# A two-layer decoder on one core: adapter scores of layer 0 issued for four groups of heads at once instead of two

## The reference

```python
# sliding-window attention, head dim 64, 8 key heads shared by 32 query heads
scores = q @ k.T * 64**-0.5 + sliding_mask          # causal, window 64
x = layernorm(x + softmax(scores) @ v @ w_out.T)
# adapter attention, head dim 8
scores  = q @ k.T / sqrt(8) + attention_mask
a_score = q @ a_k.T / sqrt(8)                       # a_k, a_v: from the context
out = softmax(scores) @ v + tanh(gate) * softmax(a_score) @ a_v
x = layernorm(x + out @ Wo)
# then 16 experts, 6 of them weighted per token, then layer 1
```

## Time and profile before

| | |
|---|---|
| Time, median of 3 runs | 1478.36 us (1475.77 to 1478.98) |
| Time of the profiled execution | 1475.77 us |
| Its span, first to last instruction | 1474.0 us |
| Mean granted TensorE clock | 0.903 of full speed |
| PE busy | 1293.9 us, 88% of the span |
| DVE busy | 1073.8 us, 73% |
| ACT busy | 687.0 us, 47% |
| Layer 0, heads phases | about 56 us in each of blocks 0 to 6, 38 us in block 7 |

### The profile page before, as it was taken

The page is one execution under the profiler, slowest core; times in us unless marked ns, Lnnn a source line. Parts: engine busy times, 40 slices in busy tenths (PEclk is TensorE's granted clock), DMA queues, the critical chain, the costliest instruction groups (busy, mean ns, idle before and its releaser), DMA issues.

```text
span 1474.0 us, 24416 instructions
## 1 busy us (share of the span) xinstructions
PE 1293.9 (88%) x9109; PEld 854.9 (58%) x9114; DVE 1073.8 (73%) x2477; ACT 687.0 (47%) x1286; POOL 102.2 (7%) x95
## 2 busy tenths in 40 slices
PE   3777999999999999999999999988899598898576
PEld 1544766766766776676676676656777322222334
DVE  3647668857857857857867865744888899999477
ACT  1323633633643543553453463432444388888242
POOL 1111011001002002001001100000000000000001
PEclk9997999999999999999999999999999855555689
DMA  8300100100200200010010013002000099999100
GB/s 334 122 11 12 60 12 15 60 12 11 64 12 4 71 12 5 24 48 12 15 60 12 12 60 115 19 22 93 8 9 5 1 182 176 176 182 171 30 1 29
DMA packets 174517, 83.96 MB, mean 57 GB/s; under 512 B 137920, under 2 KB 170048, under 8 KB 173888
## 3 DMA queue, kind: packets, MB, share of 16 engines
q1 hardware_dynamic: 173248, 82.03, 23.0%
q10 hardware_dynamic: 1152, 0.36, 0.1%
HBM read 43.57 MB, written 5.24 MB: 33 GB/s over the span
## 4 chain that ended last, share of the span: by engine, by line
PE 57%; DVE 26%; issue 6%; ACT 4%; DMA 3%; POOL 2%; SPq 0%; DVEq 0%; POOLq 0%; ACTq 0%
PE ps_t L1657 11%; PE ps_p L1641 10%; PE ps_s L1877 7%; DVE w_moe L1530 7%; PE ps_o L1779 5%; PE ps_o L1771 4%; PE ps_o L1718 4%; PE ps_o L1877 3%; PE ps_p L1695 3%; DMA w_moe<-w_moe 3%; DVE probs L1116 3%; PE ps_s L1695 2%; PE ps_o L1722 2%; DVE row_max L1122 1%; DVE w_moe L1532 1%
## 5 line engine op out<-in xcount | busy, mean ns | idle before, releaser
L1657 PE MATMUL ps_t<-ident,probs 128*128 128x128 f32 x1072 | 169.1, 279 | 28.4 <-ACT probs L844 8.2
L844 ACT ACTIVATE probs<-probs 128x512 f32<-128x512 f32 x192 | 120.7, 628 | 147.0 <-DVE probs L1116 147.0
L1657 PEld LDWEIGHTS ps_t<-ident,probs 128*128 128x128 f32 x1072 | 122.3, 141 | 78.2 <-issue 38.0
L806 ACT ACTIVATE probsT<-ps_t 128x512 f32<-128x512 f32 x232 | 136.5, 589 | 55.2 <-PE ps_t L1657 55.1
L1877 PE MATMUL ps_s<-w_moe,xbT 128*128 128x352 f32 x352 | 123.5, 476 | 0.0
L1641 PE MATMUL ps_p<-w_qkv,xinT 128*128 128x512 f32 (+1 forms) x240 | 110.2, 586 | 8.1 <-DVE ropes L1145 6.5
L2050 PEld LDWEIGHTS ps_p<-vals,w_moe 128*128 128x128 f16 x1024 | 37.5, 106 | 121.8 <-DMA w_moe<-w_moe 103.6
L759 POOL TENSOR_TENSOR rms<-mean_sq,neg_half 128x8 f32<-128x8 f32 x40 | 67.1, 1678 | 268.6 <-DVE mean_sq L1149 268.6
L806 ACT ACTIVATE bigT<-ps_t 128x512 f32<-128x512 f32 (+1 forms) x128 | 68.7, 553 | 25.4 <-PE ps_t L1657 23.4
L1877 PEld LDWEIGHTS ps_s<-w_moe,xbT 128*128 128x128 f32 x352 | 64.8, 196 | 22.7 <-issue 2.5
L1718 PE MATMUL ps_o<-v_all,probsT 128*128 128x128 f32 x512 | 71.1, 282 | 7.6 <-DVE big L1179 7.6
(11 more groups left out here) (312 smaller groups left out, 2605.8 us busy)
## 6 DMA issues: line engine op xcount, KB each, us to landing
w_out<-in_wT_out SPq DMA_DIRECT2D x8, 2048.0 KB, 8.4
w_moe<-in_wT_gu SPq DMA_DIRECT2D x1, 5632.0 KB, 19.8
w_moe<-in_wT_down SPq DMA_DIRECT2D x1, 2816.0 KB, 26.2
w_qkv<-in_wT_qkv SPq DMA_DIRECT2D x1, 2048.0 KB, 9.7
keys<-keys2T SPq DMA_DIRECT2D x8, 256.0 KB, 2.0
keys2T<-keys SPq DMA_DIRECT2D x1, 2048.0 KB, 10.6
w_moe<-w_moe SPq DMA_TRANSPOSE x128, 3.3
w_qkv<-in_wT_qkv SPq DMA_DIRECT2D x2, 512.0 KB, 8.4
```

The lines of the kernel that those rows point to most:

```text
L806: nc.scalar.activation(dst, src.bitcast(BF16) if dst.dtype == BF16 else src, ACT.Copy)\
L844: nc.scalar.activation(probs[:, at % 4, :], probs[:, at % 4, :], ACT.Exp).then_inc(L0.exped, 1)
L1657: ins = nc.tensor.transpose(dst[:, i * P:(i + 1) * P], src(i), ident_b[:] if bf else ident[:])
```

## The change

`MIXED` becomes x0 to x3, a0 to a3, x4 to x7, a4 to a7, x8 to x15. `pair_scores` is split. Sliding groups are still scored in pairs. Adapter groups are scored in fours by `adapter_scores`: head 0 of the four groups, then head 1 and so on, each of the four in its own block of 32 rows and its own bank. It waits for the reading of group `at - 1`, the one just before (`scores_read`): L0.masked for x0 to x7, L0.shifted for the others. The scores for groups at `s + 1` are issued at the end of step `s`, behind the transposes and the head sums of that step, where a pair stood at its start. In block starts they stay first, and the waits for the banks of `ps_p` and for the sliding queries move from step 1 to step 0. On DVE, where a group begins a four, the subtraction for the group before it is now issued ahead of the wait for the new scores. The number and the shapes of all instructions on every engine stay as they are.

```diff
--- before.py
+++ after.py
@@ -70,7 +70,8 @@
 
 
 
-MIXED = [("x", 0), ("a", 0), ("x", 1), ("a", 1), ("x", 2), ("a", 2), ("x", 3), ("a", 3), ("x", 4), ("x", 5), ("x", 6),
+
+MIXED = [("x", 0), ("x", 1), ("a", 0), ("a", 1), ("x", 2), ("x", 3), ("a", 2), ("a", 3), ("x", 4), ("x", 5), ("x", 6),
          ("x", 7)]
 LAST = TILES - 1
 
@@ -1096,26 +1097,31 @@
                 def scores_of(at):
                     return heads(score_bank(at), GH)
 
+                def shift():
+                    last = G0.at[ahead]
+                    q = heads(probs[:, last % 4, :], GH)
+                    if not is_masked(ahead) and last >= 4:
+                        dve.wait_ge(L0.trans, T0.done(0, ("p", *GROUPS0[last - 4])))
+                    dve.wait_ge(L0.maxed, last + 1)
+                    nc.vector.tensor_tensor(q, q if is_masked(ahead) else scores_of(last),
+                                            row_max[:, last % 4, :].unsqueeze(2).broadcast_to([P, GH, P]),
+                                            ALU.subtract).then_inc(L0.shifted, 1)
+
+
+                first_of_four = now and now[0] == "x" and now[2] % 4 == 0
+                if ahead and first_of_four:
+                    shift()
                 if now:
                     at = G0.at[now]
                     p = heads(probs[:, at % 4, :], GH)
                     dve.wait_ge(L0.scores, at + 1)
                     if is_masked(now):
                         if at >= 4:
-
                             dve.wait_ge(L0.trans, T0.done(0, ("p", *GROUPS0[at - 4])))
                         nc.vector.tensor_tensor(p, scores_of(at), mask_in[:].unsqueeze(1).broadcast_to([P, GH, P]),
                                                 ALU.add).then_inc(L0.masked, 1)
-                if ahead:
-                    last = G0.at[ahead]
-                    q = heads(probs[:, last % 4, :], GH)
-                    if not is_masked(ahead) and last >= 4:
-
-                        dve.wait_ge(L0.trans, T0.done(0, ("p", *GROUPS0[last - 4])))
-                    dve.wait_ge(L0.maxed, last + 1)
-                    nc.vector.tensor_tensor(q, q if is_masked(ahead) else scores_of(last),
-                                            row_max[:, last % 4, :].unsqueeze(2).broadcast_to([P, GH, P]),
-                                            ALU.subtract).then_inc(L0.shifted, 1)
+                if ahead and not first_of_four:
+                    shift()
                 if now:
                     if is_masked(now):
                         dve.wait_ge(L0.masked, now[1] * GX + now[2] + 1)
@@ -1666,36 +1672,55 @@
                     nc.tensor.matmul(bank.rearrange("p (a b) -> p a b", a=4), ident_b[:],
                                      ident_b[:].unsqueeze(1).broadcast_to([P, 4, P]), start=True, stop=True)
 
-            def pair_scores(first):
+            def scores_read(at):
+
+                kind, t, g = GROUPS0[at]
+                if kind == "x" and g < GX:
+                    pe.wait_ge(L0.masked, t * GX + g + 1)
+                else:
+                    pe.wait_ge(L0.shifted, at + 1)
+
+            def sliding_scores(first):
 
 
                 kind, t, g = first
                 at = G0.at[first]
                 if at >= 4:
-
-                    old = GROUPS0[at - 3]
-                    if old[0] == "x" and old[2] < GX:
-                        pe.wait_ge(L0.masked, old[1] * GX + old[2] + 1)
-                    else:
-                        pe.wait_ge(L0.shifted, at - 2)
-                if kind == "a":
-                    for j in range(2):
-                        nc.tensor.matmul(heads(score_bank(at + j), GH), ident_b[:],
-                                         mask_window[:].unsqueeze(1).broadcast_to([P, GH, P]), start=True, stop=False)
+                    scores_read(at - 3)
+                for j in range(2):
+                    nc.tensor.matmul(heads(score_bank(at + j), GH), ident_b[:],
+                                     mask_window[:].unsqueeze(1).broadcast_to([P, GH, P]), start=True, stop=False)
                 for i in range(GH):
                     for j in range(2):
                         h = g + j
-                        if kind == "a":
-                            rows = slice(HD0 * (h % 2), HD0 * (h % 2) + HD0)
-                            q, k = q0T[rows, head0(h, i) // 2, :], k0T[rows, head0(h, i) // 4, :]
-                        else:
-                            rows = slice(PAD * (h % 4), PAD * (h % 4) + HDX)
-                            place = headx(h % GX, i) // 4
-                            q, k = qkT[rows, place, :], (qkT[:, 8:16, :] if h < GX else akT)[rows, place, :]
-                        ins = nc.tensor.matmul(score_bank(at + j)[:, i * P:(i + 1) * P], q, k, start=kind == "x",
-                                               stop=kind == "x" or i == GH - 1)
+                        rows = slice(HD0 * (h % 2), HD0 * (h % 2) + HD0)
+                        ins = nc.tensor.matmul(score_bank(at + j)[:, i * P:(i + 1) * P],
+                                               q0T[rows, head0(h, i) // 2, :], k0T[rows, head0(h, i) // 4, :],
+                                               start=False, stop=i == GH - 1)
                         if i == GH - 1:
                             ins.then_inc(L0.scores, 1)
+
+            def adapter_scores(first):
+
+                kind, t, g = first
+                at = G0.at[first]
+                scores_read(at - 1)
+                for i in range(GH):
+                    for j in range(4):
+                        h = g + j
+                        rows = slice(PAD * j, PAD * j + HDX)
+                        place = headx(h % GX, i) // 4
+                        ins = nc.tensor.matmul(score_bank(at + j)[:, i * P:(i + 1) * P], qkT[rows, place, :],
+                                               (qkT[:, 8:16, :] if h < GX else akT)[rows, place, :],
+                                               start=True, stop=True)
+                        if i == GH - 1:
+                            ins.then_inc(L0.scores, 1)
+
+            def pair_scores(first):
+                if first[0] == "a":
+                    sliding_scores(first)
+                elif first[2] % 4 == 0:
+                    adapter_scores(first)
 
             def group_sum(L, b, g, dst, v):
                 pe.wait_ge(L.trans_taken, L.t.done(0, ("p", g)))
@@ -1790,7 +1815,7 @@
                 if b >= 1:
                     pe.wait_ge(hidden, E * b)
                 for s in range(len(groups) + 3):
-                    if s == 1:
+                    if s == 0:
 
                         if b >= 1:
                             pe.wait_ge(L0.proj_taken, P0.at["down", b - 1])
@@ -1800,7 +1825,8 @@
                             pe.wait_ge(L0.proj_taken, P0.done(0, ("v", 0)))
                         if mixed(b):
                             taken(L0, ("q0", b + 1, 3))
-                    if s == 0 or s % 2 == 1 and s + 1 < len(groups):
+                    turn = s == 0 or s % 2 == 1 and s + 1 < len(groups)
+                    if turn and (not s or groups[s + 1][0] == "a"):
                         pair_scores(groups[s + s % 2])
                     if s == 0 and b >= 1:
                         down_batch(b - 1, len(HB) - 1)
@@ -1823,6 +1849,9 @@
                                   ready=(L0.exped, at + 1))
                     if s >= 3:
                         head_sums(groups[s - 3])
+                    if turn and s and groups[s + 1][0] == "x":
+
+                        pair_scores(groups[s + 1])
                     for n, last in sets.items():
                         if s == last + 3:
                             sums_back(b, n)
```

## The result

| | before | changed |
|---|---|---|
| median of 4 runs, us | 1477.07 (1475.17 to 1478.98) | 1521.55 (1516.72 to 1527.14) |
| ratio, 95% interval | | 1.0301 (1.0280 to 1.0322) |
| the profiled execution, us | 1475.77 | 1516.72 |
| its span, us | 1474.0 | 1514.6 |

The change is slower by 44.5 us. The forecast was slower by 20. The measured time lies inside the range, at the upper end of it and near the time of the clock rival.

A forecast was written before the change was run, and what follows sets the result against it. Mixed blocks were taken as bound by PE and DVE handing work back and forth up to x11's subtraction, then PE; the last by PE. 7 x 3.17 - 2.4 = +20 us gave 1498 us against the median, range 1484 to 1522.

The forecast's parts named there:

- the clock rival: Mixed blocks: PE's new waits drop its clock to half, 24 us on top, 1522; chance 0.15 for over 8 us more.
- the walk of a mixed phase: Step-by-step layout of both orders' instructions in a mixed block: 3.1 to 3.2 us longer, seven of them +22.
- the mechanism of the boundaries: At x4, x8 and x12 of mixed blocks, a four waits for the group just before; each costs DVE 1.39 us.
- the last block's gain: Last block: 4.28 us of PE work go, 1.9 us of new PE waits come at its start; -2.4 us.
- What a pair of scores costs: Score matmuls: a pair takes 1.09 us on PE; a four runs in eight rounds, 1.11 us, results at 1.20.
- the rival of slow fours: Score matmuls: four row blocks don't run at once, a four takes 2.18 us; +51 us, 1529; chance 0.12.
- What is added: Mixed blocks: waits before x4, x8, x12; DVE loses 1.39 us each, PE waits 1.5 us at the first two.
- The signs asked for: Granted clock below 0.97 in blocks 1 to 6 would mean that the time went to the clock.
- PE bound all through: Rival: boundaries fall into DVE's slack, each mixed block loses 4.28 us; -32, 1446; chance 0.09 for anything faster.
- By the rule alone no block would gain: All blocks: PSUM evacuation may become the bound, so none gains; by the rows the last gains 2.4 us.

The follow-up runs named there:

- order alone: Kernel before with only the group order `MIXED` changed, scores still in pairs with the pairs' waits; 1493.92 us, ratio 1.0110.
- order and turns: Kernel before with the changed group order, scores in pairs, and sliding-output turns at steps 13, 15, 19 and 24; 1480.25 us, ratio 1.0041.
- the same, one four: Changed order, sliding-output turns at steps 13, 15, 19, 24; in mixed phases only x0 to x3 in a four, last phase in fours; 1479.02 us, ratio 1.0031.
- change, turns moved: Changed kernel with the sliding-output turns at steps 13, 15, 19 and 24 instead of 16, 17, 18 and 24; 1503.73 us, ratio 1.0186.
- change, fills: Changed kernel with four extra bf16 matmuls on PE ahead of each boundary's wait in mixed phases; 1505.93 us, ratio 1.0186.
- later fours, fills: Changed kernel in the old order; mixed phases score only x8 to x15 in fours, four extra bf16 matmuls before each four's wait; 1495.88 us, ratio 1.0148.

## Why the prediction was half right

The direction was right, and so was the mechanism of the boundaries. Three terms of the sum failed: the walk of a mixed phase lacked the waits for the two banks of `ps_t`, the last block's gain lacked a wait for the bank of the sums, and the clock, which cost most, stood outside the sum as a rival.

The phases at full clock, blocks 1 to 6, in one table:

| kernel | fours | turns | phase, us |
|---|---|---|---|
| before | none | as before | 55.6 |
| order alone | none | as before | 57.54 |
| order and turns | none | moved | 56.32 |
| the same, one four | x0 | moved | 56.32 |
| change, turns moved | all | moved | 58.11 |
| change, fills | all | as before | 59.62 |
| later fours, fills | x8, x12 | as before | 57.3 |

One half-clock stretch adds 1.5 us in the kernel of the order alone (59.05 - 57.54); in other mixed phases one added 1.0 us (59.13 against 58.11 with the turns moved) to 1.8 (61.39 against 59.62 with fills). The changed kernel's block 2 with one stretch is 61.20, so 59.7 at full clock, beside the 59.62 with fills; its other phases have two. So a typical mixed phase, 62.5 us, is 55.6 + 1.9 for the order + 2.1 for the fours + 2.8 for the clock.

- **What a pair of scores costs:** right. A four takes 1.11 us to the next turn at x8; the rival of slow fours is out.
- **What is added:** right. DVE waits 1.25 to 1.34 us at each boundary in block 1 (1.39 was the cost forecast), PE 1.33, 1.33 and 1.95. The fours' net price is 2.1 us a phase, and the experiment with one four shows that it is not their own matmuls that cost; what is left is the boundary, the wait for all four banks.
- **The walk, "a mixed block comes to 3.1 to 3.2 us longer":** this term failed. By my working after the result, which no run shows, the same walk with the order alone gives 0.9 us of it, with the fours 2.3. Measured, the fours are 2.1 and the order 1.9. The walk let every turn go as soon as its input was there; it had no wait for the two banks of `ps_t` and no look at where the moved turn of the sums would land, and moving the turns apart gave back 1.22 us of the 1.9. With that wait and ACT's copies of the sums written in, the walk gives 4.3 us, again by that working, against 59.7 - 55.6 = 4.1.
- **The last block, "-2.4 us":** failed, -0.5. The walk lacked PE's wait for ACT's copy of the sums' single bank; with two banks the 2.8 us less than before are there (35.36 against 38.15).
- **The clock:** given 0.15 as a rival at "14 x 1.7 = 24", it happened, and it is the largest missing term: eleven stretches in the phases of blocks 1 to 6, where before has none. The six phases together are 15.8 us over six times 59.65, so a stretch cost about 1.4 us; block 0 has three more. The signs asked for were there: a granted clock of 0.95 in block 1, "below 0.97". The forecast took rows 8 (waits of 0.82 and 0.47 us, then a clock of 0.50) for a mild risk, although it put two waits of 1.5 us into each phase. The Trainium skill ("TensorE: Matmul & The Clock Gate", A second HAM failure mode: psum-queue depth-cycling) describes a kernel whose TensorE idles briefly between groups and so swings between the two clocks. The traces here agree in part: half clock came behind waits of 0.6 to 1.9 us, but not behind all of them.
- **PE bound all through:** out. With the turns moved PE was busy 48.72 us at full clock against 52.99 before, and the phase took 58.11 us against 55.61.
- **"By the rule alone no block would gain":** the rule of the Trainium skill ("TensorEngine Tiling (Array Packing)", PSUM Bottleneck) is that the copy out of PSUM may become the bound once tiling has made TensorE faster. The last block agrees with it in part: PE waited 2.1 us for a PSUM bank to be emptied, though ACT, which empties it, was busy only 21 of 37.65 us, and DVE's 11 us of slack did not help.
- **A reading:** "DVE 40.57" in block 1 is the column of PE's weight loads; DVE was busy 41.34 us. So DVE idles 14.5 us there and not 15; nothing in the sum uses it.

Open: what decides whether the clock falls behind a wait. In block 1 a wait of 1.33 us had half clock behind it at x4 and full clock at x8, the 1.61 us wait of the order alone had none, and in that kernel the same two waits had half clock behind them in one phase and not in another. Not tried: an order that puts masked groups ahead of every four, whose banks come free one step earlier.

## What to carry to other kernels

Work that needs several banks at once waits for the last of them; ask first whether the time saved was on the path, then price the wait, then the clock behind the wait, which here cost more than the wait did (2.8 us against 2.1 in a typical mixed phase). When groups are moved in an order that a table of steps refers to, list what lands on the same step and which banks it shares. If an engine's waits can't be removed, filling them with idle matmuls can be worth it, and its price shows once the waits are short.

## What the hardware showed

- Four score matmuls, one on each block of rows with 128 columns and a bank each, start within 0.02 us, and the rounds of four records follow every 0.11 us, as rounds of two did: sixteen matmuls take 1.11 us to the next transposes, eight in pairs 1.09.
- A stretch at half clock of 3.4 us costs 1.5 us in phases whose PE is busy 91% of the time (59.05 against 57.54), and between 1.0 and 1.8 in other mixed phases; in the last phase one cost nothing (37.64 against 37.65), and two in a row 1.2 or 3.1. It appeared within the same execution in some phases and not in others that issue the same instructions.
- Less work on TensorE can take longer: the last phase took 34.28 us with 31.51 us busy at clock 1.00, and 37.81 with 30.57 busy at 0.91. How much of that is the clock and how much the fours' waits is not shown; 6.8 us of half clock cost 1.2 to 3.1 us in that phase elsewhere.
